# Graph attention on one core: VectorE scales all eight tiles of gathered rows, ScalarE none

## The chip, the core and the metric

One core of one Trainium2 chip runs the whole program in one launch. The core's engines work side by side and are ordered only by semaphores: TensorE (PE), VectorE (DVE), ScalarE (ACT), GpSimd (POOL) and SyncE (SP). The metric is the device time of one execution in microseconds, the median of several. All data are float32.

## The reference

There are 6250 nodes with 256 features and 106,250 edges (the last 6250 are loops), sorted by destination. First a convolution over the edges, `x = x + conv(relu(layernorm(x)))`. Then two layers of graph attention (GAT) on `relu(layernorm(x))`, with 4 heads of 64 features:

```python
z = (x @ W).reshape(n, HEADS, ODIM)
el = jnp.sum(z * al, axis=-1)
er = jnp.sum(z * ar, axis=-1)
e = jax.nn.leaky_relu(el[src] + er[dst], negative_slope=NEG_SLOPE)
e_max = jax.ops.segment_max(e, dst, num_segments=n)
ex = jnp.exp(e - e_max[dst])
denom = jax.ops.segment_sum(ex, dst, num_segments=n)
msg = z[src] * (ex / denom[dst])[:, :, None]
out = jax.ops.segment_sum(msg, dst, num_segments=n)
```

and `elu(out + x + b)` after that. The output is the sum of the convolution's result and the second layer's.

## The kernel before

The program has a front stage (layer norm, tables of the nodes, tables of the groups), a convolution stage and two GAT stages, one for each layer (`gat_stage`). The change touches the GAT stages alone.

The edges lie in 104 groups of 1024, each of 8 tiles of 128 edges, one edge on each partition. One step v of a GAT stage works on one group. Four steps make a quad (r = 0 to 3), and `all_steps` loops over the quads and writes out the last one behind the loop. Between the steps' work on edges each quad also finishes one block of 256 nodes: reciprocals of the denominators in r=0, `node_state` in r=0, ScalarE's exponentials of the ELU in r=1, VectorE's `elu` in r=2, table rows for the next layer (layer 0) or the output (layer 1) in r=2 and 3.

A step's work, with its lines:

- GpSimd (L1669 to L1675) issues 8 gathers, one for each tile, in the order of tiles 0, 2, 4, 6 and then 1, 3, 5, 7. Each is an indirect DMA that reads 128 indices from on-chip memory and brings 128 rows of 264 numbers into the buffer `zg[r]`. There are four buffers. The even tiles of group v+4 may be gathered once TensorE has summed the even tiles of group v (`half_summed`), the odd ones once it has summed the odd ones (`part_summed`). The convolution stage has its own gathers (L1111).
- VectorE builds one-hot matrices (L859 to L871), adds the two score parts (L1892, it waits for the gathered rows), and takes the running maxima by scans within the tiles (L1902, L1903), over the tiles (L1909, L1910) and back (L1916 to L1926), with small transposes by TensorE in between (L1715, L1723, L1729). It subtracts the maximum (L1931), and ScalarE takes the exponentials (L1619), which land in the gathered rows as four numerators for each edge.
- The rows are scaled, each head's 64 features by its numerator. The even tiles are VectorE's: `scale_even_rows(v + 1)` runs in step v, a step ahead, in two operations of 128x512 (L1938), two tiles each. The odd tiles are ScalarE's: in step v itself, 16 activations of 128x64 (L1635), one for each of 4 tiles and 4 heads, each with the numerator as its scale. Their last one counts up `rows_act_ready`.
- TensorE sums rows into 4 x 32 places with the one-hots, even tiles first and odd tiles later in its order (`tile_sums`, L1748). Between the halves stand `hand_back` (L1723), `spread_er` and `block_er` (L1695). ScalarE copies the sums out (L1640), TensorE moves them to the nodes' places (`window_sums`), and VectorE adds them in the next step (L1949 to L1958).

VectorE's order in step v is: `over_tiles(v+1)`, adding of window v-1, denominators or elu, one-hots of v+3, `into_tiles` and `finish_tiles` of v+1, scores of v+2, `differences(v+1)`, `scale_even_rows(v+1)`, `within_tiles(v+2)`, and in r=0 `node_state`. The order of each engine is written out by hand.

Of the kernel before, what the change touches and what calls it, by code (L numbers as in the profile page):

```python
# [20 lines left out]
ACT = mybir.ActivationFunctionType  # L21
# [6 lines left out]
D = 256  # L28
MUL = 64
HEADS = 4  # L30
# [1350 lines left out]
def gat_stage(nc, m, layer):  # L1381
# [8 lines left out]
    with ExitStack() as ctx:  # L1390
# [17 lines left out]
        def scratch(width, parts=P):  # L1408
# [60 lines left out]
        got = [sem(f"gathered{r}") for r in range(4)]  # L1469
        (sp_done, pe_go, idx_ready, staged_ready, pool_go, rel_ready, hot_ready, pick_ready, hotT_ps, hotT_ready, er4_ps, er4_ready,  # L1470
         er_ready, raw_ready, score_ready, eT_ready, ends_ready, lv_ready, state_ready, ini_ready, init_ready, fwd_ready,
         max_ready, maxT_ready, diff_ready, ex_ready, rows_scaled, rows_act_ready, half_summed, part_summed, sums_ready, scaled,
         summed, added) = [
            sem(n) for n in ("sp_done", "pe_go", "idx_ready", "staged_ready", "pool_go", "rel_ready", "hot_ready", "pick_ready",
                             "hotT_ps", "hotT_ready", "er4_ps", "er4_ready", "er_ready", "raw_ready", "score_ready",
                             "eT_ready", "ends_ready", "lv_ready", "state_ready", "ini_ready", "init_ready", "fwd_ready",
                             "max_ready", "maxT_ready", "diff_ready", "ex_ready", "rows_scaled", "rows_act_ready",
                             "half_summed", "part_summed", "sums_ready", "scaled", "summed", "added")]
        block = ctx.enter_context(nc.Block())

# [9 lines left out]
        def numerators(r):  # L1490

            return zg[r].rearrange("p (k w) -> p k w", w=ZW)[:, :, D:D + HEADS]

        def head_rows(r, k, h):

            at = k * ZW + h * HF
            return zg[r][:, at:at + HF]

        @block.sync
        def _(sp):  # L1500
# [82 lines left out]
        @block.scalar  # L1583
        def _(act):
            last_quad = load_last_quad(act, m)

            def copy_hotT(v):
                act.wait_ge(hotT_ps, v + 1)
                nc.scalar.copy(hotT, ps_hotT[:, 0:2 * P]).then_inc(hotT_ready, 1)

            def exponential(k, b=node):
                act.wait_ge(s_v, k + 1)
                nc.scalar.activation(b.h, b.x, ACT.Relu, scale=-1.0).then_inc(s_neg, 1)
                act.wait_ge(s_neg, k + 1)
                nc.scalar.activation(b.h, b.h, ACT.Exp, scale=-1.0).then_inc(s_ex, 1)
                act.wait_ge(s_ex, k + 1)
                nc.scalar.activation(b.ps[:, :], b.h, ACT.Copy, bias=-1.0).then_inc(s_em, 1)

            def rows(k, t):
                act.wait_ge(s_pZ, k * 2 + (t + 1))  # L1600
                if t == 0:
                    act.wait_ge(st_rows, k * 16 + 16)
                nc.scalar.copy(node.rows[:, t * ZW:(t + 1) * ZW], ps_node[:, 0:ZW]).then_inc(s_rows, 1)

            def last_rows(k, t, b):
                act.wait_ge(s_pZ, k * 2 + (t + 1))
                if t == 0 and b is node:
                    act.wait_ge(st_rows, k * 16 + 16)
                nc.scalar.copy(b.rows[:, t * ZW:(t + 1) * ZW], b.tables[t][:, 0:ZW]).then_inc(s_rows, 1)

            groups = [stage_sources(nc, act, m, r, idx[r], idx_ready) for r in range(4)]
            for r in range(4):
                stage_places(nc, act, m, r, groups[r], staged[r], columns[r], staged_ready)
            for v in range(2):
                copy_hotT(v)

            def exponentials(v, r, u):
                act.wait_ge(diff_ready, v + 1)
                nc.scalar.activation(numerators(r), lanes(diff[u]), ACT.Exp).then_inc(ex_ready, 1)  # L1619
                nc.scalar.activation(fac[u][:, :], m.fac_mask[:, :], ACT.Exp, bias=fd[u][:, 0:1]).then_inc(ex_ready, 1)  # L1620

            exponentials(0, 0, 0)

            def step(quad, r, ahead):
                v = quad * 4 + r
                u = r % 2
                if ahead >= 2:
                    copy_hotT(v + 2)
                if ahead >= 4:
                    group = stage_sources(nc, act, m, v + 4, idx[r], idx_ready)  # L1630
                act.wait_ge(ex_ready, v * 2 + 2)
                for k in range(1, G, 2):
                    for h in range(HEADS):
                        at = k * ZW + D + h
                        ins = nc.scalar.activation(head_rows(r, k, h), head_rows(r, k, h), ACT.Copy,  # L1635
                                                   scale=zg[r][:, at:at + 1])
                ins.then_inc(rows_act_ready, 1)
                act.wait_ge(part_summed, v + 5)
                act.wait_ge(summed, v + 1)
                nc.scalar.copy(sums, ps_part[:, 0:D + HEADS]).then_inc(sums_ready, 1)  # L1640
                if ahead >= 1:
                    exponentials(v + 1, (r + 1) % 4, 1 - u)
                if r == 1:
                    exponential(quad)
                if r >= 2 and layer == 0:
                    rows(quad, r - 2)
                if ahead >= 4:
                    act.wait_ge(pick_ready, v + 1)
                    stage_places(nc, act, m, v + 4, group, staged[r], columns[r], staged_ready)

            all_steps(act, last_quad, step)
            first, lead = load_rest(act, m, last_quad)
            with act.Fori(first, REAL, 2) as n:
                k = n + lead
                exponential(k)
                exponential(k + 1, second)
                if layer == 0:
                    for t in range(2):
                        last_rows(k, t, node)
                    for t in range(2):  # L1660
                        last_rows(k + 1, t, second)
# [19 lines left out]
        def _(pe):  # L1681
# [57 lines left out]
            def tile_sums(v, r, q):  # L1739

                if q == 0:
                    pe.wait_ge(rows_scaled, v + 1)
                    pe.wait_ge(sums_ready, v + 1)
                else:
                    pe.wait_ge(rows_act_ready, v + 1)
                for j in range(NB):
                    k = 2 * j + q
                    ins = nc.tensor.matmul(ps_part[j * TW:(j + 1) * TW, 0:D + HEADS], one_hot(r, k),  # L1748
                                           zg[r][:, k * ZW:k * ZW + D + HEADS], start=(q == 0), stop=(q == 1),
                                           skip_group_check=True)  # L1750
                return ins
# [106 lines left out]
        def _(dve):  # L1858
# [78 lines left out]
                by = by_tile[:, :, D:D + HEADS].rearrange("p k (h o) -> p k h o", o=1)  # L1937
                return V.tensor_tensor(rows, rows, by.broadcast_to([P, len(range(first, last, 2)), HEADS, HF]), ALU.mult)  # L1938

            def scale_even_rows(v, r):  # L1940
                dve.wait_ge(ex_ready, v * 2 + 1)
                scale_rows(r, 0, NB)
                scale_rows(r, NB, G).then_inc(rows_scaled, 1)

            def scale_first(v, u, base):
                dve.wait_ge(summed, v + 2)
# [72 lines left out]
            one_hots(2, 2)  # L2019
            scores(1, 1, 16 * G)  # L2020
            place_er(2)
            scale_even_rows(0, 0)
            within_tiles(1, 1, 32)

            slot = Mem()

            def step(quad, r, ahead):
                v = quad * 4 + r
                u = r % 2
                if r == 0:  # L2030
                    slot.n = load_block(dve, m, quad)
                if r == 0:
                    slot.base = load_base(dve, m, v - 1)
                base = slot.base
                if ahead >= 1:
                    over_tiles(v + 1, 1 - u)
                scale_first(v - 1, 1 - u, base)
                add_window(v - 1, 1 - u, base)
                if r == 0:
                    denominators(slot.n, quad, quad * 4 + 2)  # L2040
                if r == 2:
                    elu(quad)
                if r == 3 and layer == 1:
                    output(quad, quad * 16 + 16)
                if ahead >= 3:
                    one_hots(v + 3, (r + 3) % 4)
                node_picks(v, r)
                if ahead >= 1:
                    into_tiles(v + 1, 1 - u)
                if ahead >= 3:  # L2050
                    place_er(v + 3)
                if ahead >= 1:
                    finish_tiles(v + 1, 1 - u)
                if ahead >= 2:
                    scores(v + 2, (r + 2) % 4, quad * 128 + (128 if r < 2 else 256))
                if r < 3:
                    slot.base = load_base(dve, m, v)
                if ahead >= 1:
                    differences(v + 1, 1 - u)
                    scale_even_rows(v + 1, (r + 1) % 4)  # L2060
                if ahead >= 2:
                    within_tiles(v + 2, u, quad * 64 + ((r + 2) // 2 + 1) * 32)
                if r == 0:
                    node_state(slot.n, quad, quad * 16 + 16)
                    if layer == 0:
                        clear_sums(slot.n)
# [77 lines left out]
```

## Time and profile before

| what | us |
|---|---|
| timed runs, median of 3 | 3518.95 (3518.66 to 3522.92) |
| profiled execution, its span | 4581.9 |
| its own time beside the span | not given |
| convolution's gathers, first to last start | 107.5 to 1805.8 |
| GAT's gathers, first to last start | 1851.0 to 4528.9 |
| mean granted clock of TensorE | 0.611 |

The span is 1063 us longer than the timed runs, so a duration in the profile can be set beside the timed run only with care. Busy time is the sum of the recorded durations of an engine, "idle before" the time in which the engine did nothing just before instructions of that line, with what ended it.

### The profile page before, as it was taken

The page shows a single profiled execution, that of the slowest core. Times are in us where ns is not written, and L with a number is a line of the kernel's source. Part 1 is how long each engine was busy: PE and PEld are TensorE (multiplying, and loading weights), DVE is VectorE, ACT ScalarE, POOL GpSimd, SP SyncE. Part 2 cuts the span into 40 slices and gives each one's busy share as a digit, 9 for nine tenths or more (in the row PEclk, how much of TensorE's full clock was granted, in tenths as well). Part 3 has the DMA queues.
Part 4 walks back from the last instruction along what each step waited for, and adds up shares of the span by engine and source line. Part 5 has one row for each costly group of instructions (what it writes and reads, how often), then busy time and mean ns, then how long its engine had stood idle before and what let it go on. Part 6 is the DMA issues. An engine that isn't in the chain of part 4 may idle for free. (4 is left out here: it accounts for less than half of the span.)

```text
span 4581.9 us, 78327 instructions
## 1 busy us (share of the span) xinstructions
PE 3134.4 (68%) x20204; PEld 1904.6 (42%) x20205; DVE 2415.9 (53%) x7011; ACT 1756.2 (38%) x6334; POOL 2565.8 (56%) x2634
## 2 busy tenths in 40 slices
PE   7677777667677777477767776776466667666666
PEld 5344444344444444244444444444244334433433
DVE  6444554444455445355555555555355555555555
ACT  6122211121222122355555554554345445554554
POOL 6554444444444443566666666663566666666663
PEclk8777777777777777555555555555555555555555
DMA  7222222222222222333333333332333333333332
GB/s 238 84 86 83 81 81 81 78 80 85 82 80 82 82 85 74 99 102 103 102 105 101 103 102 106 100 102 76 99 101 101 106 105 100 101 109 100 102 101 81
DMA packets 241741, 442.78 MB, mean 97 GB/s; under 512 B 83665, under 2 KB 134933, under 8 KB 241567
## 3 DMA queue, kind: packets, MB, share of 16 engines
q0 software_dynamic: 119808, 334.13, 26.7%
q1 hardware_dynamic: 121887, 108.14, 7.7%
q8 instruction: 16, 0.26, 0.0%
q14 instruction: 30, 0.25, 0.0%
HBM read 381.95 MB, written 60.10 MB: 96 GB/s over the span
## 5 line engine op out<-in xcount | busy, mean ns | idle before, releaser
L1673 POOL DMA_INDIRECT nodes<-z_rows,scratch x1664 | 1674.4, 1006 | 1048.6 <-issue 501.9
L1111 POOL DMA_INDIRECT scratch<-h_rows,scratch x832 | 817.1, 982 | 892.7 <-DVE nodes L1261 676.2
L1635 ACT ACTIVATE nodes<-nodes 128x64 f32<-128x64 f32 x3328 | 816.3, 333 | 6.2 <-issue 6.2
L1155 PE MATMUL ce_part<-nodes,scratch 128*32 128x128 f32 (+1 forms) x6656 | 459.4, 391 | 151.0 <-issue 133.9
L1748 PE MATMUL ge_part<-nodes,scratch 128*32 128x260 f32 x3328 | 449.9, 633 | 5.7 <-ACT nodes L1635 5.7
L1640 ACT COPY scratch<-ge_part 128x260 f32<-128x260 f32 x208 | 78.1, 375 | 958.2 <-issue 635.0
L1909 DVE TENSOR_TENSOR_SCAN scratch<-scratch,ge_runs 1x36 f32<-1x36 f32 x208 | 45.1, 217 | 755.3 <-remote 685.7
L1723 PE MATMUL ge_runs<-ident,scratch 1*36 1x1 f32 x832 | 76.4, 192 | 527.9 <-DVE scratch L1910 491.9
L1289 DVE TENSOR_TENSOR nodes<-nodes,ce_sum 128x512 f32 x105 | 72.3, 689 | 660.7 <-remote 389.9
L1155 PEld LDWEIGHTS ce_part<-nodes,scratch 128*32 128x32 f32 x6656 | 254.9, 139 | 360.3 <-issue 299.0
L1135 PE MATMUL ce_w<-fc_sb,scratch 64*128 64x256 f32 x1664 | 313.1, 507 | 107.6 <-ACT scratch L1030 95.4
L1261 DVE TENSOR_TENSOR nodes<-ce_w,scratch 128x768 f32<-128x768 f32 x416 | 376.9, 947 | 0.0
L1723 PEld LDWEIGHTS ge_runs<-ident,scratch 1*36 1x36 f32 x832 | 64.3, 154 | 700.0 <-issue 700.0
L1069 ACT COPY nodes<-ce_part 128x512 f32<-128x512 f32 x104 | 60.9, 585 | 759.6 <-remote 663.9
L1165 PE MATMUL ce_sum<-nodes 128*128 128x128 f32 x832 | 157.7, 348 | 231.2 <-issue 167.6
L1938 DVE TENSOR_TENSOR nodes<-nodes 128x512 f32<-128x512 f32 x416 | 269.7, 690 | 66.5 <-issue 46.5
L1135 PEld LDWEIGHTS ce_w<-fc_sb,scratch 64*128 64x128 f32 x1664 | 188.1, 243 | 279.3 <-issue 197.3
L1758 PE MATMUL ge_sum<-scratch 128*128 128x128 f32 x832 | 247.3, 451 | 20.1 <-ACT scratch L1640 10.2
L1030 ACT ACTIVATE scratch<-ce_hid 128x512 f32<-128x512 f32 x104 | 62.1, 597 | 510.3 <-PE ce_hid L1124 478.9
L1695 PE MATMUL ge_hotT<-scratch 128*128 128x4 f32 x416 | 121.8, 363 | 192.5 <-issue 104.1
L1165 PEld LDWEIGHTS ce_sum<-nodes 128*128 128x128 f32 x832 | 133.4, 244 | 273.8 <-issue 197.7
L1702 PE MATMUL ge_er<-scratch 128*128 128x16 f32 x832 | 215.5, 380 | 0.9 <-issue 0.9
(271 smaller groups left out, 5538.3 us busy)
## 6 DMA issues: line engine op xcount, KB each, us to landing
nodes<-z_rows,scratch POOLq DMA_INDIRECT x1664
nodes<-hT SPq DMA_DIRECT2D x56, 256.0 KB
scratch<-h_rows,scratch POOLq DMA_INDIRECT x832
z_rows<-scratch SPq DMA_DIRECT2D x28, 264.0 KB
z_rows<-nodes SPq DMA_DIRECT2D x28, 264.0 KB
hT<-scratch SPq DMA_DIRECT2D x28, 256.0 KB
hT<-nodes SPq DMA_DIRECT2D x28, 256.0 KB
nodes<-x_rows SPq DMA_DIRECT2D x28, 256.0 KB
```

The source lines that it names most:

```text
L1111: nc.gpsimd.indirect_dma_start(xg[u][:, i * D:(i + 1) * D], None, m.h_rows, bass.IndirectOffsetOnAxis(ap=idx[r][:, k:k + 1], axis=0)).then ...
L1135: ins = nc.tensor.matmul(ps_w[q][:, 2 * half + a, :, :].rearrange("p k f -> p (k f)"), hidT[u][rows, col:col + P], m.fc1[rows, :], start=T ...
L1155: ins = nc.tensor.matmul(here, hots[u][:, at:at + TW], these, start=(q == 0 and c == 0), stop=(q == 1), skip_group_check=True)
L1165: ins = nc.tensor.matmul(ps_sum[:, c, :], sums[:, c * P:(c + 1) * P], pick[u], start=(c == 0), stop=True, skip_group_check=True)
L1261: ins = V.tensor_tensor(out[:, :, 1 + 3 * k:4 + 3 * k, :], w[:, :, 2 + k:3 + k, :].broadcast_to([P, UNIT, 3, MUL]), x[:, :, 1:4, :], ALU.mult)
L1635: ins = nc.scalar.activation(head_rows(r, k, h), head_rows(r, k, h), ACT.Copy, scale=zg[r][:, at:at + 1])
L1673: nc.gpsimd.indirect_dma_start(zg[r][:, k * ZW:(k + 1) * ZW], None, m.z_rows[layer], bass.IndirectOffsetOnAxis(ap=idx[r][:, k:k + 1], axis ...
L1702: ins = nc.tensor.matmul(ps_er[:, q * W:(q + 1) * W], hotT[:, q * P:(q + 1) * P], er4, start=(q == 0), stop=True, skip_group_check=True)
L1723: ins = nc.tensor.matmul(ini[:, k:k + 1], state[:, k * LANES:(k + 1) * LANES], m.ident[0:1, 0:1], start=(k == 0), stop=True, skip_group_ch ...
L1748: ins = nc.tensor.matmul(ps_part[j * TW:(j + 1) * TW, 0:D + HEADS], one_hot(r, k), zg[r][:, k * ZW:k * ZW + D + HEADS], start=(q == 0), st ...
L1758: nc.tensor.matmul(ps_sum[u][:, c * NW:(c + 1) * NW], sums[:, c * P:(c + 1) * P], pick[u], start=False, stop=True, skip_group_check=True)
L1938: return V.tensor_tensor(rows, rows, by.broadcast_to([P, len(range(first, last, 2)), HEADS, HF]), ALU.mult)
```

## The change

ScalarE's loop over the odd tiles goes, with its semaphore `rows_act_ready` and its helper. VectorE's `scale_even_rows` becomes `scale_half`, called twice in each step: for the even tiles where it stood, and for the odd tiles of the same group behind `within_tiles(v + 2)`, and in r=0 ahead of `node_state`. Each call is two operations of 128x512. `rows_scaled` counts both halves, and TensorE waits for the half that it sums.

```diff
@@ scalar
-                act.wait_ge(ex_ready, v * 2 + 2)
-                for k in range(1, G, 2):
-                    for h in range(HEADS):
-                        at = k * ZW + D + h
-                        ins = nc.scalar.activation(head_rows(r, k, h), head_rows(r, k, h), ACT.Copy,
-                                                   scale=zg[r][:, at:at + 1])
-                ins.then_inc(rows_act_ready, 1)
                 act.wait_ge(part_summed, v + 5)
@@ tensor
                 if q == 0:
-                    pe.wait_ge(rows_scaled, v + 1)
                     pe.wait_ge(sums_ready, v + 1)
-                else:
-                    pe.wait_ge(rows_act_ready, v + 1)
+                pe.wait_ge(rows_scaled, v * 2 + (q + 1))
@@ vector
-            def scale_even_rows(v, r):
-                dve.wait_ge(ex_ready, v * 2 + 1)
-                scale_rows(r, 0, NB)
-                scale_rows(r, NB, G).then_inc(rows_scaled, 1)
+            def scale_half(v, r, q):
+                if q == 0:
+                    dve.wait_ge(ex_ready, v * 2 + 1)
+                scale_rows(r, q, NB + q)
+                scale_rows(r, NB + q, G).then_inc(rows_scaled, 1)
@@ ahead of the steps
-            scale_even_rows(0, 0)
+            scale_half(0, 0, 0)
             within_tiles(1, 1, 32)
+            scale_half(0, 0, 1)
@@ step
                     differences(v + 1, 1 - u)
-                    scale_even_rows(v + 1, (r + 1) % 4)
+                    scale_half(v + 1, (r + 1) % 4, 0)
                 if ahead >= 2:
                     within_tiles(v + 2, u, quad * 64 + ((r + 2) // 2 + 1) * 32)
+                if ahead >= 1:
+                    scale_half(v + 1, (r + 1) % 4, 1)
                 if r == 0:
                     node_state(slot.n, quad, quad * 16 + 16)
```

## Rows read from the trace of the kernel before

**Rows 1.** The page's head: span, then busy time, share of the span, instructions.
```profile
span 4581.9 us, 78327 instructions
PE 3134.4 (68%) x20204; PEld 1904.6 (42%) x20205; DVE 2415.9 (53%) x7011; ACT 1756.2 (38%) x6334; POOL 2565.8 (56%) x2634
```
**Rows 2.** Costliest groups: line, engine, operation, count | busy us, mean ns | idle before, releaser.
```profile
L1673 POOL DMA_INDIRECT nodes<-z_rows,scratch x1664 | 1674.4, 1006 | 1048.6 <-issue 501.9
L1111 POOL DMA_INDIRECT scratch<-h_rows,scratch x832 | 817.1, 982 | 892.7 <-DVE nodes L1261 676.2
...
L1909 DVE TENSOR_TENSOR_SCAN scratch<-scratch,ge_runs 1x36 f32<-1x36 f32 x208 | 45.1, 217 | 755.3 <-remote 685.7
...
L1289 DVE TENSOR_TENSOR nodes<-nodes,ce_sum 128x512 f32 x105 | 72.3, 689 | 660.7 <-remote 389.9
...
L1938 DVE TENSOR_TENSOR nodes<-nodes 128x512 f32<-128x512 f32 x416 | 269.7, 690 | 66.5 <-issue 46.5
```
**Rows 3.** The two gather lines alone: shortest, median, longest ns; first and last start.
```profile
L1673 POOL DMA_INDIRECT nodes<-z_rows,scratch x1664: 947/953/1592, 1851.0 to 4528.9; - x185
...
L1111 POOL DMA_INDIRECT scratch<-h_rows,scratch x832: 947/953/1355, 107.5 to 1805.8; - x167
```
**Rows 4.** Gathers in order of time: start us, us, line, count, idle before and releaser.
```profile
1850.95 0.95 POOL L1673 DMA_INDIRECT nodes<-z_rows,scratch  x1 [44.23 <-ACT scratch L841]
...
2422.83 0.96 POOL L1673 DMA_INDIRECT nodes<-z_rows,scratch  x1 [0.30 <-issue]
...
3221.96 0.95 POOL L1673 DMA_INDIRECT nodes<-z_rows,scratch  x1 [61.52 <-ACT scratch L841]
```
**Rows 5.** L1938's pairs and gathers started under them: first, four steps, last.
```profile
1887.89 1.25 POOL L1673 DMA_INDIRECT nodes<-z_rows,scratch  x1 [0.30 <-issue]
...
2409.14 1.29 DVE L1938 TENSOR_TENSOR nodes<-nodes 128x512 f32<-128x512 f32 x2 [0.32 <-issue]
...
2409.94 1.32 POOL L1673 DMA_INDIRECT nodes<-z_rows,scratch  x1 [0.30 <-issue]
...
2419.15 1.29 DVE L1938 TENSOR_TENSOR nodes<-nodes 128x512 f32<-128x512 f32 x2 [0.32 <-issue]
...
2419.83 1.44 POOL L1673 DMA_INDIRECT nodes<-z_rows,scratch  x1 [0.30 <-issue]
...
2430.40 1.29 DVE L1938 TENSOR_TENSOR nodes<-nodes 128x512 f32<-128x512 f32 x2 [0.32 <-ACT nodes L1619]
...
2430.77 1.15 POOL L1673 DMA_INDIRECT nodes<-z_rows,scratch  x1 [0.30 <-issue]
...
2443.97 1.29 DVE L1938 TENSOR_TENSOR nodes<-nodes 128x512 f32<-128x512 f32 x2 [0.32 <-issue]
...
2444.39 1.09 POOL L1673 DMA_INDIRECT nodes<-z_rows,scratch  x1 [0.30 <-issue]
...
4512.60 1.45 POOL L1673 DMA_INDIRECT nodes<-z_rows,scratch  x1 [0.30 <-issue]
```
**Rows 6.** The same four steps in order of time: first scans, L1903, L1635, L1748, L1715.
```profile
2401.84 0.22 DVE L1909 TENSOR_TENSOR_SCAN scratch<-scratch,ge_runs 1x36 f32<-1x36 f32 x1 [5.58 <-remote]
...
2414.46 0.22 DVE L1909 TENSOR_TENSOR_SCAN scratch<-scratch,ge_runs 1x36 f32<-1x36 f32 x1 [0.52 <-PE ge_runs L1715]
...
2420.76 0.38 DVE L1903 TENSOR_TENSOR_SCAN scratch<-scratch,ge_eT 36x128 f32<-36x128 f32 x1
...
2422.29 3.92 ACT L1635 ACTIVATE nodes<-nodes 128x64 f32<-128x64 f32 x16
...
2424.51 0.22 DVE L1909 TENSOR_TENSOR_SCAN scratch<-scratch,ge_runs 1x36 f32<-1x36 f32 x1 [3.37 <-remote]
...
2427.40 1.10 PE L1748 MATMUL ge_part<-nodes,scratch 128*32 128x260 f32 x8
...
2434.10 0.40 PE L1715 MATMUL ge_runs<-perm,scratch 36*1 36x36 f32 x4
...
2446.53 0.39 DVE L1903 TENSOR_TENSOR_SCAN scratch<-scratch,ge_eT 36x128 f32<-36x128 f32 x1
```

More of the change, by code:

```diff
@@ L1471, in gat_stage @@
          er_ready, raw_ready, score_ready, eT_ready, ends_ready, lv_ready, state_ready, ini_ready, init_ready, fwd_ready,
-         max_ready, maxT_ready, diff_ready, ex_ready, rows_scaled, rows_act_ready, half_summed, part_summed, sums_ready, scaled,
+         max_ready, maxT_ready, diff_ready, ex_ready, rows_scaled, half_summed, part_summed, sums_ready, scaled,
          summed, added) = [
@@ L1476, in gat_stage @@
                              "eT_ready", "ends_ready", "lv_ready", "state_ready", "ini_ready", "init_ready", "fwd_ready",
-                             "max_ready", "maxT_ready", "diff_ready", "ex_ready", "rows_scaled", "rows_act_ready",
+                             "max_ready", "maxT_ready", "diff_ready", "ex_ready", "rows_scaled",
                              "half_summed", "part_summed", "sums_ready", "scaled", "summed", "added")]
@@ L1492, in numerators @@
             return zg[r].rearrange("p (k w) -> p k w", w=ZW)[:, :, D:D + HEADS]
-        def head_rows(r, k, h):
-            at = k * ZW + h * HF
-            return zg[r][:, at:at + HF]
         @block.sync
```

## The prediction

> **What bounds the kernel now.** I read the page's head first, then the costliest groups, then the first and last starts of the two gather lines, then single gathers in order of time.
>
> The head shows no full engine: PE 68%, GpSimd (POOL) 56%, VectorE (DVE) 53%, ScalarE (ACT) 38% [rows 1]. It also shows a span of 4581.9 us, while the timed runs have a median of 3518.95 us. The profile gives no other time for that execution, so 1063 us of the span are time that an unprofiled run does not spend. Where they lie: DVE stands idle 685.7 us before L1909 (GAT) and 389.9 us before L1289 (convolution), put down to "remote", which no engine of this kernel can be [rows 2]. Together that is 1075.6 us, about the difference: I read it as stops that come with the recording. So neither shares nor the chain of waits may be read as the timed run's bound. What can be read are durations and back-to-back rates.
>
> The one that adds up is GpSimd. One gather takes 953 ns in the median (1006 in the mean in the GAT stages, 982 in the convolution) [rows 2, 3] and the next starts 0.30 us after it even when nothing is waited for [rows 4]. The sum, if GpSimd never waited for a buffer in the timed run:
> - gathers: 1674.4 + 817.1 = 2491.5 us [rows 2]
> - gaps: about 2490 x 0.305 = 760 us [rows 4]
> - before the first gather 107.5 us, between convolution and GAT 44.2, between the layers 61.5, after the last gather 4581.9 - 4528.9 - 0.95 = 52.0 [rows 1, 3, 4]: 265 us
>
> Together 3516 us, against 3518.95 measured. I take it that the timed run is bound by the issue of gathers from end to end. In the GAT stages that is 208 steps x 8 x (1.006 + 0.305) = 2181 us, 10.5 us a step.
>
> **The change, part by part.**
>
> *ScalarE loses 16 activations a step*, 3.92 us, 208 x 3.92 = 815 us busy [rows 6]. They lie beside the gathers. TensorE's odd tile sums waited for them; now they wait for DVE's second half, which was done in the step before. GpSimd may gather for step v+4 once the tile sums of v are done, and the scores that need these rows come two steps and some 3 us later: about 23 us for 10.5 us of gathers. So an earlier release of buffers is worth nothing as long as GpSimd is the bound. I cost it at 0.
>
> *VectorE gains 416 operations* of 128x512, the same form as L1938 (690 ns) [rows 2]. A pair takes 1.29 us [rows 5]: 208 x 1.29 = 268 us more busy time. Is there room? I rebuild DVE's steps without the unexplained idle. Step r=0: 2401.84 to 2414.46, 12.6 us. Step r=1: 2414.46 to the end of L1903 at 2421.14, and 0.5 to the next scan, 7.2. Step r=2: 2424.51 until PE's L1715 has ended at 2434.50, and 0.5, 10.5. Step r=3 like r=1 with a table multiplication on PE, about 8.2 [rows 6]. Four steps: 38.5 us, against 4 x 10.5 = 42.0 for GpSimd. The new pair stands behind L1903, where DVE anyway waits for PE to transpose ends: 1.29 less the 0.5 of that wait is 0.8 in r=1 and in r=3 (or less, behind the table multiplication); nothing in r=2, where PE sets the end; up to 1.3 in r=0, where node_state fills the wait already. Of 2.9 I take 2.5. So DVE's chain goes to about 41.0 us. Queued behind the pair are node_state (r=0) and the next step's two short scans, for which PE's hand_back waits; they have 42 us. Cost 0; if that cover is gone, up to 2.5 us in four steps, 52 times: 130 us.
>
> *What the pair does to GpSimd.* A gather whose start falls inside an L1938 operation is lengthened, until that operation is nearly over: in four successive steps the pairs at 2409.14, 2419.15, 2430.40 and 2443.97 have one gather start each under them, and it takes 1.32, 1.44, 1.15 and 1.09 us instead of 0.95, so 0.37, 0.49, 0.20 and 0.14 us more, 0.30 a pair [rows 5]. In both layers 163 gathers are lengthened in this way, by 57.3 us together, 0.276 for each of the 208 pairs; the first and the last of them stand in [rows 5] too. This is most of the 1674.4 - 1664 x 0.953 = 88.6 us that gathers take over their median [rows 2, 3]. The reason is arithmetic: a pair (1.29 us) is as long as the gathers' period (1.257), so each pair catches one start. ScalarE's activations lengthen none: the gather at 2422.83 lies within a burst of them (from 2422.29, 3.92 us) and takes 0.96 [rows 4, 6]. The second pair catches one more start a step. Bounds: 0 (it always falls into the gap between two operations or is over) and 0.57 (a start right at an operation's beginning; estimated from the 0.69 of one operation less the 0.12 us before its end at which the gather at 2409.94 got through: 0.80 + 0.37 = 1.17 us after a pair of 1.29). I take the measured mean, 0.276. Since GpSimd is the bound, it adds in full: 208 x 0.276 = 57 us.
>
> A page has this mechanism: the Trainium skill, "SBUF — State Buffer", section "Who interferes with whom", says that a DVE instruction with two SBUF inputs contends with a GpSimd instruction that reads SBUF, and that the one that comes second waits for the other altogether. The trace agrees for the gather. It does not for DVE: by that rule an L1938 that starts in a gather would wait for up to 0.95 us, but 690 ns is its mean. By the whole rule DVE would lose up to 0.5 us a pair more, which would lead to the third case below.
>
> *Waits that go or move:* ScalarE's wait for ex_ready (its own earlier work) and PE's rows_act_ready: 0. The drain and the first step of each layer gain or lose under 2 us.
>
> The sum: 3516 + 57 = 3573 against the profile's sum, and carried to the median, 3518.95 + 57 = 3576 us.
>
> **The rivals.**
>
> 1. *ScalarE or the engines' ring was the bound, not GpSimd (faster).* In step r=1 ScalarE also does the node's exponentials; its scaling ends at 2426.21, 11.75 us after that step's start. DVE and PE, without the idle, would be there after 7.2 us of this step and 2.9 of the next (the odd sums at 2427.40 less the scan at 2424.51), 10.1 us. So ScalarE is late by 1.6 us once in four steps [rows 6]. For it: 38.5 + 1.6 = 40.1 is near GpSimd's bare 4 x 8 x 1.257 = 40.2, and the gap of 0.30 us might be shorter unprofiled. Against it: the sum above matches to 3 us, and DVE's chain grows by 2.5 as ScalarE's 1.6 goes. If it decides: at most 1.6 x 52 = 83 us less, 3436; half of it, about 3475, since the gathers take over as the bound.
>
> 2. *The collisions do not add (same).* The gathers of a step are in a fixed phase to DVE; behind a gather held by the first pair the next one starts 1.26 us later, perhaps ahead of the second pair, which may end before another start. By hand: a held gather gets through 0.57 or 1.18 us after the pair's start (the end of either operation less 0.12), so the next one starts at 1.83 or 2.43 and the one after at 3.09 or 3.69. The second pair begins at L1903's end, D behind the first, and holds what starts from D to D + 0.57 and from D + 0.61 to D + 1.18. D is 2.0 in one step (2421.14 - 2419.15) and 2.95 in another (2446.92 - 2443.97) [rows 5, 6]. With 2.0 the two phases lose 0.09 and 0.14, with 2.95 they lose 0.43 and 0.44. The mean of the four is 0.28, so I do not believe it. Or GpSimd has slack in every step that takes the 0.28. Time 3519.
>
> 3. *VectorE becomes the bound (slower by more).* Decides if DVE's four steps were really at 42 and not at 38.5 us before, or if DVE is held by gathers too. Then 2.4 us in four steps, 52 times, 125 us: 3644.
>
> That the change doesn't do what it says: it does; the diff removes every ScalarE scaling, and half 1 reads the same numerators.
>
> **How the numbers follow.** Forecast (collisions, GpSimd bound) 0.50; rival 1 0.22; rival 2 0.15; rival 3 0.13. 0.2% of 3519 is 7 us, about what can be told from no change. Faster 0.22, same 0.15, slower 0.63. The likeliest case alone has 3540 to 3600 (0.1 to 0.4 us a step). The range reaches half into rival 1 and to most of rival 3: 3470 to 3635.
>
> **What would show it.** Right: no L1635; L1938's line with 832 operations of about 690 ns; the gather's median still 953 ns and its mean up by 0.276/8 = 35 ns to about 1040; about twice as many gathers above 1.0 us; the second pair with one lengthened gather under it. DVE's idle before L1909 shrinks. The profiled span says little, it may even fall, as 16 x 208 recorded instructions go. Wrong: a mean of the gathers at 1006 with the time up (then rival 3), or a time below 3510 (then rival 1, and ScalarE's end of scaling must have stood late in the chain).

## The result, and the profile after

The changed kernel takes 3569.52 us in the median (3567.22 to 3571.95), the one before on the same chip 3520.84. The ratio is 1.0144 (95% interval 1.013 to 1.0159): slower by 48.7 us, where 57 was forecast. "On-chip memory" is below, as in the prediction, SBUF, where the gathered rows lie; PSUM is the separate memory that TensorE writes its sums to.

First the page of the changed kernel: head, then the two gather lines, the scaling line and the line that waits for gathered rows, answering to [rows 1, 2] (L1661 was L1673, L1924 was L1938, L1878 was L1892).

```profile
span 3567.2 us, 75207 instructions
...
PE 2865.9 (80%) x20204; PEld 1774.6 (50%) x20205; DVE 2640.9 (74%) x7427; ACT 949.0 (27%) x3006; POOL 2653.8 (74%) x2634
...
L1661 POOL DMA_INDIRECT nodes<-z_rows,scratch x1664 | 1743.4, 1048 | 588.8 <-issue 454.7
L1111 POOL DMA_INDIRECT scratch<-h_rows,scratch x832 | 836.2, 1005 | 264.5 <-issue 246.5
L1924 DVE TENSOR_TENSOR nodes<-nodes 128x512 f32<-128x512 f32 x832 | 532.7, 680 | 66.6 <-ACT nodes L1614 66.6
...
L1878 DVE TENSOR_TENSOR scratch<-nodes,ge_er 128x32 f32<-128x32 f32 x208 | 39.5, 190 | 394.2 <-DMA nodes<-z_rows,scratch 394.2
```

This profile has the length of the timed runs; the one before had 1063 us more. So its rows can't be set against [rows 1, 2] as they stand. A second profile of the kernel before, taken among the experiments, has 3512.9 us and no stops. Its answering rows:

```profile
span 3512.9 us, 78327 instructions
...
PE 2820.0 (80%) x20204; PEld 1753.3 (50%) x20205; DVE 2414.7 (69%) x7011; ACT 1748.0 (50%) x6334; POOL 2592.9 (74%) x2634
...
L1673 POOL DMA_INDIRECT nodes<-z_rows,scratch x1664 | 1684.7, 1012 | 594.5 <-issue 467.2
L1111 POOL DMA_INDIRECT scratch<-h_rows,scratch x832 | 834.0, 1002 | 264.3 <-issue 248.2
L1635 ACT ACTIVATE nodes<-nodes 128x64 f32<-128x64 f32 x3328 | 816.6, 333 | 0.2 <-issue 0.2
...
L1892 DVE TENSOR_TENSOR scratch<-nodes,ge_er 128x32 f32<-128x32 f32 x208 | 39.4, 190 | 431.3 <-DMA nodes<-z_rows,scratch 430.1
```

No busy share in either shows the bound. The last row of each does: VectorE waits 430 and 394 us for gathered rows, and most of GpSimd's idle time before a gather is put down to "issue" (467.2 of 594.5 us and 454.7 of 588.8), the 0.30 us behind each gather. Whatever a gap is put down to, none between two gathers of one GAT stage is longer than 0.32 us in either kernel.

The gathers account for the difference. The busy time of those in the GAT stages grew by 1743.4 - 1684.7 = 58.7 us, the span by 54.3. Most of the rest is between the layers, where GpSimd waits 48.38 us before and 44.65 us after for the second layer's first indices:

```profile
2387.13 0.95 POOL L1673 DMA_INDIRECT nodes<-z_rows,scratch  x1 [48.38 <-ACT scratch L841]
```

```profile
2405.54 0.95 POOL L1661 DMA_INDIRECT nodes<-z_rows,scratch  x1 [44.65 <-ACT scratch L841]
```

One step of the changed kernel, in order of time (start, duration), shows where gathers lose it:

```profile
2049.56 0.95 POOL L1661 DMA_INDIRECT nodes<-z_rows,scratch  x1 [0.30 <-issue]
...
2050.06 1.29 DVE L1924 TENSOR_TENSOR nodes<-nodes 128x512 f32<-128x512 f32 x2 [0.32 <-ACT nodes L1614]
...
2050.82 1.35 POOL L1661 DMA_INDIRECT nodes<-z_rows,scratch  x1 [0.30 <-issue]
...
2051.97 1.26 DVE L1924 TENSOR_TENSOR nodes<-nodes 128x512 f32<-128x512 f32 x2
...
2052.48 0.98 POOL L1661 DMA_INDIRECT nodes<-z_rows,scratch  x1 [0.30 <-issue]
...
2056.28 1.50 POOL L1661 DMA_INDIRECT nodes<-z_rows,scratch  x1 [0.30 <-issue]
...
2056.54 0.41 DVE L864 TENSOR_TENSOR scratch<-cols,scratch 128x256 f32<-128x256 f32 x1
```

The gather at 2050.82 starts 0.76 us into the first pair and is let through at 2051.22, 0.13 us before the pair's end. "Let through" means here the gather's recorded end less the 0.95 us that an undisturbed one takes. The next starts 1.257 us behind that, at 2052.48, 0.51 us into the second pair, just before the gap between its two operations, and loses only 0.03. The one at 2056.28 is held by the one-hot operations, which also read two operands from on-chip memory: it is let through at 2056.83, 0.12 us before the end of L864's.

"Hold" is, from here on, the busy time of the GAT stages' gathers less 1664 x 0.953 us.

### The profile page after: what moved, and what is told of

It is laid out like the page before. It is cut to its first block and busy times, and to the rows that moved or that the text cites. A ratio compares the mean times of both kernels' runs of the same rounds, so it can differ in the third digit from the quotient of the medians.

```text
span 3567.2 us, 75207 instructions
## 1 busy us (share of the span) xinstructions
PE 2865.9 (80%) x20204; PEld 1774.6 (50%) x20205; DVE 2640.9 (74%) x7427; ACT 949.0 (27%) x3006; POOL 2653.8 (74%) x2634
## 5 line engine op out<-in xcount | busy, mean ns | idle before, releaser
L1661 POOL DMA_INDIRECT nodes<-z_rows,scratch x1664 | 1743.4, 1048 | 588.8 <-issue 454.7
L1924 DVE TENSOR_TENSOR nodes<-nodes 128x512 f32<-128x512 f32 x832 | 532.7, 680 | 66.6 <-ACT nodes L1614 66.6
L1155 PE MATMUL ce_part<-nodes,scratch 128*32 128x128 f32 (+1 forms) x6656 | 316.7, 339 | 73.9 <-DVE nodes L1261 73.3
L1878 DVE TENSOR_TENSOR scratch<-nodes,ge_er 128x32 f32<-128x32 f32 x208 | 39.5, 190 | 394.2 <-DMA nodes<-z_rows,scratch 394.2
L1155 PEld LDWEIGHTS ce_part<-nodes,scratch 128*32 128x32 f32 x6656 | 202.7, 122 | 183.2 <-DVE nodes L1261 90.8
L1259 DVE TENSOR_TENSOR nodes<-ce_w,scratch 128x512 f32<-128x512 f32 x208 | 143.2, 688 | 104.9 <-DMA scratch<-h_rows,scratch 86.4
L1696 PE MATMUL ge_eT<-ident,scratch 128*36 128x128 f32 x208 | 78.8, 379 | 155.8 <-DVE scratch L1881 154.0
L1683 PEld LDWEIGHTS ge_hotT<-scratch 128*128 128x128 f32 x416 | 104.3, 311 | 196.0 <-issue 120.5
L1690 PEld LDWEIGHTS ge_er<-scratch 128*128 128x128 f32 x832 | 193.4, 323 | 4.9 <-ACT scratch L1584 1.7
L1744 PEld LDWEIGHTS ge_sum<-scratch 128*128 128x128 f32 x832 | 187.1, 312 | 6.5
L1614 ACT ACTIVATE nodes<-scratch 128x32 f32<-128x32 f32 x208 | 53.5, 257 | 474.3 <-DVE scratch L1917 474.3
```

What stands on the lines that cost most here:

```text
L1155: ins = nc.tensor.matmul(here, hots[u][:, at:at + TW], these, start=(q == 0 and c == 0), stop=(q == 1), skip_group_check=True)
L1259: V.tensor_tensor(out[:, :, 0:8:7, :], w[:, :, 0:2, :], x[:, :, 0:1, :].broadcast_to([P, UNIT, 2, MUL]), ALU.mult)
L1661: nc.gpsimd.indirect_dma_start(zg[r][:, k * ZW:(k + 1) * ZW], None, m.z_rows[layer], bass.IndirectOffsetOnAxis(ap=idx[r][:, k:k + 1], axis ...
L1683: nc.tensor.matmul(ps_er4, selT, erw[r], start=True, stop=True).then_inc(er4_ps, 1)
L1690: ins = nc.tensor.matmul(ps_er[:, q * W:(q + 1) * W], hotT[:, q * P:(q + 1) * P], er4, start=(q == 0), stop=True, skip_group_check=True)
L1744: nc.tensor.matmul(ps_sum[u][:, c * NW:(c + 1) * NW], sums[:, c * P:(c + 1) * P], pick[u], start=False, stop=True, skip_group_check=True)
```

## The experiments

Theory A: gathers set the time, and VectorE's operations with two on-chip operands hold them. Theory B: VectorE's added work is the cost. Theory C: ScalarE's scaling, or the ring of waits between the engines that runs through it, sets the step.

| kernel | time us | ratio to before (95%) | profiled span | GAT gathers' busy | hold | span less hold |
|---|---|---|---|---|---|---|
| before, second profile | 3514.8 (one run) | | 3512.9 | 1684.7 | 98.9 | 3414.0 |
| e1 | 3512.96 | 0.9976 (0.9966 to 0.9986) | 3511.5 | 1689.9 | 104.1 | 3407.4 |
| changed | 3569.52 | 1.0144 (1.013 to 1.0159) | 3567.2 | 1743.4 | 157.6 | 3409.6 |
| e2 | 3426.81 | 0.9732 (0.9716 to 0.9748) | 3426.0 | 1601.7 | 15.9 | 3410.1 |
| e3 | 3659.82 | 1.0405 (1.038 to 1.0429) | 3660.3 | 1837.9 | 252.1 | 3408.2 |
| e4 | 3478.33 | 0.9887 (0.9869 to 0.9906) | 3474.2 | 1644.3 | 58.5 | 3415.7 |
| e5 | 3705.21 | 1.0523 (1.0501 to 1.0545) | 3706.1 | 1878.9 | 293.1 | 3413.0 |
| e6 | 3508.46 | 0.9968 (0.9954 to 0.9982) | 3499.6 | 1671.9 | 86.1 | 3413.5 |

The last column is the finding: eight kernels whose spans lie 280 us apart all have 3411 us, to within 5, once the hold is taken off. About half of what is left of the spread is the gap between the layers: 48.4 and 48.3 us in the two kernels in which ScalarE scales the odd tiles (before, e4), 43.8 to 45.4 in the other six.

**The kernel before again, for a profile.** No edit.

> The kernel before, unchanged, for a second profile: the first one's span is 1063 us over its timed runs, the changed kernel's is not. Theory A (gathers are the bound, and an operation of VectorE that reads two operands from on-chip memory holds a gather that starts under it): if this profile has the timed length (3519 to 3530 us), GpSimd's gathers follow each other without a wait in the GAT stages, 10.6 us a step, and their mean is near 1.02 us, of which L1938's pairs account for about 0.3 us a step. Theory B (VectorE's added work is what costs): GpSimd shows waits for tile sums between gathers, and gathers are not continuous. If the span is again near 4580 us, the stops belong to how this kernel is recorded and nothing is told apart.

As theory A has it: gathers without a gap, mean 1.012 us, 10.62 us a step in the first layer (1234.7 to 2337.8, 831 intervals, times 8) and 10.46 in the second. L1938's pairs hold 68 us of the 98.9, 0.33 a step. The first profile's stops belong to that recording.

**e1: ScalarE scales almost nothing.** One head of one odd tile is still scaled; the other 15 blocks of the odd rows stay unscaled, so the output is not the reference's.

```diff
-                for k in range(1, G, 2):
-                    for h in range(HEADS):
+                for k in (7,):
+                    for h in (3,):
```

> The kernel before, in which ScalarE scales one head of one tile instead of 16 blocks in each step: the other odd rows stay unscaled, so this part of the computation is left out. Theory A: ScalarE is not in the way, time within 0.2% of before (3512 to 3526 us). Theory C (ScalarE's scaling or the ring through it sets the step): 30 to 80 us faster than before.

8 us below before in the timed runs, 1.4 us in the spans. Taking away 15 of 16 activations is worth 0.24% (0.34% at most by the interval), not 30 to 80 us: theory C falls. It is also slightly more than the 0.2% that A allowed. The gap between the layers is 4.6 us shorter than in the second profile of before (43.78 against 48.38), which may be the larger part of it; the rest stays open.

**e2: the changed kernel, numerators in PSUM.** The work stays with VectorE, one operand moves; ScalarE has one activation more a step.

```diff
+        num = [ps_er[:, 256 + TR * u:256 + TR * (u + 1)] for u in range(2)]
...
                 act.wait_ge(diff_ready, v + 1)
+                nc.scalar.activation(num[u].rearrange("p (k h) -> p k h", k=G), lanes(diff[u]), ACT.Exp)
...
+            act.wait_ge(raw_ready, 2)
             exponentials(0, 0, 0)
...
-                by = by_tile[:, :, D:D + HEADS].rearrange("p k (h o) -> p k h o", o=1)
+                by = num[r % 2].rearrange("p (k h o) -> p k h o", k=G, o=1)[:, first:last:2]
```

> The changed kernel, in which VectorE reads the numerators of all four scaling operations from PSUM (ScalarE writes them there too, one activation of 128x32 more a step), so the operations have one operand in on-chip memory. VectorE's count and order of work are unchanged. Theory A: no gather is held by them; the gathers' mean in the GAT stages falls from 1.048 to about 0.98 us and the time by 117 us from 3569, to 3440 to 3465 us. Theory B: VectorE's time is as it was, so the time stays at 3555 to 3580 us. A variant of A in which a scaling operation holds the gather by its write and not by its second read: also 3555 to 3580 us, with gathers still lengthened.

3426.8 us: 142.7 us below the changed kernel, and 2.7% below before. VectorE's operations are as long (673 against 680 ns) and as many:

```profile
L1664 POOL DMA_INDIRECT nodes<-z_rows,scratch x1664 | 1601.7, 963 | 588.9 <-issue 491.1
...
L1927 DVE TENSOR_TENSOR nodes<-nodes,ge_er 128x512 f32<-128x512 f32 x832 | 527.4, 673 | 97.1 <-ACT nodes L1616 97.1
```

And gathers that start under them are not held:

```profile
2055.62 1.28 DVE L1927 TENSOR_TENSOR nodes<-nodes,ge_er 128x512 f32<-128x512 f32 x2 [0.47 <-ACT nodes L1616]
...
2056.15 0.95 POOL L1664 DMA_INDIRECT nodes<-z_rows,scratch  x1 [0.30 <-issue]
...
2057.41 0.95 POOL L1664 DMA_INDIRECT nodes<-z_rows,scratch  x1 [0.30 <-issue]
...
2057.53 1.25 DVE L1927 TENSOR_TENSOR nodes<-nodes,ge_er 128x512 f32<-128x512 f32 x2
...
2058.67 0.95 POOL L1664 DMA_INDIRECT nodes<-z_rows,scratch  x1 [0.30 <-issue]
```

Theory B falls, and so does the variant in which the write holds: the operations still write on-chip memory. The Trainium skill, "SBUF — State Buffer", section "Who interferes with whom", says just this: an instruction of VectorE with at most one on-chip input, outside the modes that use both ports, does not contend with GpSimd. The trace agrees, 0.95 us for the gathers above. The gain went beyond the 104 to 129 us expected, because the one-hots' hold fell too, from 38 to 13 us. Their operations are unchanged, but they hold 55 gathers instead of 105: the gathers meet them at another moment.

**e3: the odd half in one operation of 1024.**

```diff
+                if q == 1:
+                    scale_rows(r, 1, G).then_inc(rows_scaled, 1)
+                    return
```

> The changed kernel, in which the odd half is one operation of 128x1024 instead of two of 128x512: VectorE's work is a little smaller (about 0.04 us a step). Theory A: a gather that starts under it waits for up to 1.1 us instead of up to 0.57, so the second half costs about twice as much: 40 to 80 us slower than 3569, 3610 to 3650 us, with gathers of up to 2.1 us. Theory B: 0 to 10 us faster than 3569.

90 us slower than the changed kernel, 10 more than expected at most, with less work on VectorE (247.7 us for 208 operations of 1024 in place of 262 for the two). Gathers are let through 1.07 us after its start, instead of 0.53: 74 that started just ahead of it lose 1.16 us each, 130 that started half-way lose 0.50 to 0.56.

```profile
2060.81 1.19 DVE L1924 TENSOR_TENSOR nodes<-nodes 128x1024 f32<-128x1024 f32 x1
...
2061.32 1.51 POOL L1661 DMA_INDIRECT nodes<-z_rows,scratch  x1 [0.30 <-issue]
```

**e4: the kernel before, numerators in PSUM** (e2's edit on the kernel before; ScalarE keeps the odd tiles).

> The kernel before (VectorE scales the even tiles, ScalarE the odd ones), with VectorE's numerators read from PSUM as in the second experiment. Theory A: with no hold by a scaling operation, who scales the odd tiles no longer matters: the gathers' mean is 0.96 us and the time 3415 to 3435 us, within 0.3% of the 3427 us of the changed kernel with PSUM numerators. Theory B (part of the cost is VectorE's time, hidden so far behind the larger one): clearly below it, 3400 us or less.

A miss for theory A: 3478 us, 51 us above e2. No scaling operation holds a gather (mean 0.988), but the one-hot operations hold 144 of them, by 57.9 us; in e2 it is 55, by 13.3. So 43 of the 48 us between the two spans are hold. Who scales the odd tiles matters after all, by the phase in which it puts the one-hots to the gathers, that is, by the moment within them at which gathers start. Theory B is not what remains: VectorE does more work in e2, which is the faster.

**e5: the odd half in four operations of 256.**

```diff
+                if q == 1:
+                    for k in range(1, G, 2):
+                        ins = scale_rows(r, k, k + 1)
+                    ins.then_inc(rows_scaled, 1)
+                    return
```

> The changed kernel, in which the odd half is four operations of 128x256 (one tile each) instead of two of 128x512. VectorE's work grows by some 0.1 to 0.2 us a step. Theory A: a gather that starts under one of them waits for up to 0.23 us instead of 0.57; the 49 us that the second half takes from the gathers fall to 15 to 25, the time to 3535 to 3555 us. Theory B: the time goes up by 5 to 30 us, 3575 to 3600.

The largest miss: 3705 us, slower by 136 where a gain was expected. The gathers' mean is 1.129, so it is hold, not VectorE's work. The profile shows why:

```profile
2054.62 1.40 DVE L1924 TENSOR_TENSOR nodes<-nodes 128x256 f32<-128x256 f32 x4
...
2055.14 1.72 POOL L1661 DMA_INDIRECT nodes<-z_rows,scratch  x1 [0.30 <-issue]
```

The gather starts 0.52 us into the four and is let through at 2055.91, 1.29 us in, just before the last one ends. None gets in between. Of the 208 fours, 137 have a gather start 0.5 to 0.6 us into them, all let through at 1.27 to 1.28, and 65 have one start just ahead of them, which loses 1.36 us: 89 of the 194 us that the fours hold. The operations follow each other at 0.32 to 0.34 us and each lasts 0.40. Those of 512 mostly follow at 0.58 to 0.62 and last 0.66 to 0.70, and there gathers are let through in the middle, at 0.53 to 0.57. What decides between the two spacings was not tried.

**e6: odd half right behind the even half.**

```diff
+                if ahead >= 1:
+                    scale_half(v + 1, (r + 1) % 4, 1)
                 if ahead >= 2:
                     within_tiles(v + 2, u, quad * 64 + ((r + 2) // 2 + 1) * 32)
-                if ahead >= 1:
-                    scale_half(v + 1, (r + 1) % 4, 1)
```

> The changed kernel, in which the odd half stands right behind the even half, ahead of the scans within tiles, so four operations of 128x512 follow each other for 2.5 us. VectorE's count is unchanged, but what TensorE waits for comes 1.29 us later. Theory A with the phases as I have them: a gather let through 0.57 us after the first start has its follower at 1.83, just as the fourth operation begins, which is held for the full 0.57; one let through at 1.18 has it at 2.43, nearly free. Some more hold than with the halves apart: 3565 to 3620 us. If holds do not depend on the order of the operations: 3569. Theory B: a longer chain, 3590 to 3640 us, with gathers of unchanged mean (1.048).

A miss in direction: 3508 us, 61 below the changed kernel and 0.3% below before, with the same instructions.

```profile
2049.54 2.57 DVE L1924 TENSOR_TENSOR nodes<-nodes 128x512 f32<-128x512 f32 x4 [0.32 <-ACT nodes L1614]
...
2050.13 0.95 POOL L1661 DMA_INDIRECT nodes<-z_rows,scratch  x1 [0.30 <-issue]
...
2051.39 0.95 POOL L1661 DMA_INDIRECT nodes<-z_rows,scratch  x1 [0.30 <-ACT scratch L841]
```

The gather at 2050.13 hits the gap between the first two operations (0.59 us in) and the next, 1.257 later, the gap ahead of the fourth (1.85). Operations 0.60 apart have gaps 1.2 apart, and gathers come 1.257 apart: one that is let through in a gap brings its follower into another. I had called a start at 1.83 the beginning of a hold; it is the last moment that is free. The third and fourth operation hold 2 gathers in all 208 steps, by 1.3 us.

## Why the prediction was right, and where it was off

*GpSimd is the bound.* Right. The sum of 3516 us, made from a profile 1063 us too long, stands beside a second profile of 3512.9 in which gathers never wait within a stage. That the sum came within 3 us of the timed run was in part luck: in the second profile all gathers, the convolution's too, are busy for 2518.7 us and not 2491.5, and the stretches before, between and after the stages are 234 us and not 265, so two errors of about 30 us cancelled. The 88.6 us that the GAT stages' gathers took above the median were 98.9 there.

*ScalarE's activations are worth nothing (rival 1 has them as the bound).* Right to 0.24% (e1). They may be worth about 4 us between the layers, where GpSimd waits 48 us with them and 44 to 45 without.

*VectorE's time is hidden.* Right. The scaling line is busy for 262 us more and the engine, whose neighbouring operations overlap, for 226; yet e2, with all of that work, has a span less hold of 3410.1, the changed kernel 3409.6 and the kernel before 3414.0. Rival 3 falls with it.

*The second pair costs what the first does, 0.276 us a step.* The mechanism was right and the size near. The second pair holds 51 us, 0.245 a step. But not as a copy of the first: 58 of the 208 second pairs hold a gather by 0.61 to 0.63 us, one that started 0.1 us ahead of them, which is above the 0.57 that I gave as the upper bound; 99 meet one at 0.50 to 0.55 us and take 0.02; 34 meet one at 0.05 to 0.27 us and take 0.27 to 0.44; the others lie between or meet none. So 94 second pairs hold a gather noticeably, not each of them, as the prediction's sign had it. 36 of the 51 us come from the gathers that started ahead, which by the prediction's rule (a start inside the pair) would not be held at all. That the sum came out near the mean is luck to that extent. A phase that puts all starts in a gap (e6) would have given 0, and one operation of 1024 (e3) three times as much. The one-hots hold 10 us more than before (38 against 27), which I did not foresee. Hold as a whole grew by 58.7 us; less the shorter gap between the layers (3.7 us) that is near the 54.3 between the spans. The timed medians lie 48.7 apart: the run profiled for the second time took 3514.8 us, 4 less than the fastest of those behind the median of before.

*The gathers' mean to about 1040 ns.* 1048, against 1012 in the second profile of before: up by 36, forecast 35. Gathers above 1.0 us: 364 against 238, not twice as many.

*Rival 2 (holds do not add)* was refused by a calculation whose cases were too coarse: D, the time from the first pair's start to the second's, was 1.91 us in most steps, not 2.0 to 2.95. With 1.91 its own rule gives 0 for one phase and 0.05 for the other, which would have spoken for this rival; what it lacked is the hold of a gather that starts ahead of the pair. e6 shows that this rival can be made true by order alone.

*VectorE is not held by gathers.* Right but for a remainder. The prediction looked for up to 0.95 us and found none in the mean. Single starts show up to 0.07 us: when a gather starts up to 0.045 us behind a first pair's beginning, it is not held and the operation takes up to 0.77 us instead of 0.69; from 0.047 us on the operation takes 0.69 and the gather is held (second profile of before, changed kernel, e3 and e6, some forty cases of the first kind). Both kinds, from the changed kernel:

```profile
1560.84 1.36 DVE L1924 TENSOR_TENSOR nodes<-nodes 128x512 f32<-128x512 f32 x2 [0.32 <-ACT nodes L1614]
1560.87 0.96 POOL L1661 DMA_INDIRECT nodes<-z_rows,scratch  x1 [0.30 <-issue]
...
1603.71 1.29 DVE L1924 TENSOR_TENSOR nodes<-nodes 128x512 f32<-128x512 f32 x2 [0.32 <-ACT nodes L1614]
1603.76 1.47 POOL L1661 DMA_INDIRECT nodes<-z_rows,scratch  x1 [0.31 <-issue]
```

*The profiled span may fall.* It did, by 1015 us, but the second profile of before shows that this says nothing of the change.

## What to carry to other kernels

Where GpSimd issues gathers back to back and they set the time, an operation on VectorE with two on-chip operands is paid for even where VectorE has 26% of its time free: count how many gather starts fall under it or just ahead of it, and for how long. Move one operand to PSUM before moving work between engines; here this turned a change that cost 1.4% into one that gains 2.7%. It gained only 1.1% on the kernel before (e4), since what other operations hold depends on the phase, and order alone was worth 61 us (e6): read the hold again after each move. Cutting an operation into pieces helps only if gathers get in between the pieces, which in e5, at 256 elements, they did not.

## What the runs showed of the hardware

- A gather under such an operation is let through 0.12 to 0.13 us before its end (0.57 of 0.69, 1.07 of 1.19), and under four short ones only so long before the last one's end (1.27 of 1.40).
- In the changed kernel, the twelve gathers that started between 0.045 us ahead of and 0.038 us behind the beginning of a first pair, which had waited for a semaphore, were not held, and the pair's first operation took up to 0.76 us instead of 0.69. The 58 that started 0.1 us ahead of a second pair, which was queued behind scans, were held, by 0.62 us. I had taken an operation's recorded start as the start of its hold. Why it differs between the two pairs was not tried.
- One profile of the kernel before had 1063 us of stops that its second one and the timed runs lack, while the durations agree: 953 ns for the median gather in both.
